# One propagation table with a shared block of fixed rows, and separate 96-wide store tiles in the first dense pass

## The chip, the cores and the metric

The kernel runs on one core of a Trainium2 chip. The metric is the device time of one execution in microseconds; all arithmetic is float32.

## The reference

Four graph layers run one after the other on 50,000 nodes of 96 features with 50,000 edges sorted by destination. Each layer works on `h = relu(layernorm(x))` and adds its result to `x`.

```python
h = relu(layernorm(x));  x = x + attention(h, edges, edge_attr_96)      # L0: 8 heads, sums over edges per destination
h = relu(layernorm(x));  x = x + gated_messages(h, edges, edge_attr_32) # L1: two small networks per edge, update network, layernorm
h = relu(layernorm(x));  x = x + propagate(h, edges)                    # L2: K = 16 rounds
h = relu(layernorm(x));  x = x + gcn(h, edges, edge_weight, W, b)       # L3
# L2, with norm from the in-degrees of both ends and a self loop on each node:
for _ in range(16):
    h = 0.9 * segment_sum(norm * h[row], col) + 0.1 * h_start
```

A node without an incoming edge has only its self loop in L2, so its value never changes over the rounds.

## The kernel before, in words

**Layout.** Every per-node or per-edge list is padded to `ROWS` = 128 x 392 rows: partition p holds 392 consecutive ones, worked on in 49 batches (`NB`) of 8 columns (`J`), that is 1,024 rows or 384 KB a batch. Nodes that have incoming edges are kept a second time in "slots", one per edge position (`SLOTS` = 128 x 400 rows), where the sum of a destination's edges ends up. A table that is gathered from holds first the `ROWS` fixed rows and behind them the `SLOTS` slots. `row_e` holds, for each edge, the row of its source in such a table: below `ROWS` for a node whose value is fixed, `ROWS` + slot for one that changes.

**Stages.** The program is a row of blocks; in each the five queues (SyncE for DMAs, GpSimd for gathers and scatters, TensorE, ScalarE, VectorE) run their own skewed loop (`skewed`: stage function with lag n works on batch t - n in tick t). Semaphores order them; between two blocks all engines meet. SyncE waits for its last stores before it leaves a block. The blocks, with the prefix of their tile names:

- `n`: first layer norm, keys and values (gathers of x).
- `d`, lines 722 to 952, called here the first dense pass: L0 projection of edge features, and, for the nodes as if they had no edge, the L1 update, its layer norm, the sum `x2` and the start value `y0` of L2. GpSimd scatters pointers into `kv_t`. One tile `d_yx`, 192 columns a row, holds `y0` in columns 0 to 95 and `x2` in 96 to 191. The SyncE function `store` writes `x2` to `x2n_t` and `y0` to both tables `y_t[0]` and `y_t[1]`.
- `e0`, `e1`: edge passes of L0 and L1. `e1` stores the start values of the slots into `y_t[1]`.
- `r0` with `d3`: round 0 of L2 (gathers from `y_t[1]`, stores slots to `y_t[0]`) beside the dense part for nodes with fixed values, which loads `y0` from the fixed rows of `y_t[0]`.
- `r`: rounds 1 to 14. GpSimd gathers the source rows of a batch (8 `indirect_dma_start` of 128 rows of 384 bytes) from one table, VectorE scans them, TensorE and ScalarE form the new values in `H`, SyncE stores these to the slots of the other table; a round starts gathering when all stores of the one before have landed.
- `l`, `e3`: round 15 with the L3 product, and the last edge pass with the scatter of the output.

In the first dense pass ScalarE does per tick two groups of 8 `ACTIVATE` of 128x96 (`norm`, `norm2`, line 354), two Gelu (line 876), two copies out of PSUM (`turned`, line 869), two roots (line 341), two table loads and the two copies that set up the scatter (862, 863). TensorE does transposes into `d_te` (line 824), which need the ScalarE copy before them, then the products `d_pu` (line 832), which the Gelu waits for.

`ptr_e` (pointers read back in `e0`) and `src_i` (source indices) are whole-list tiles that nothing uses behind `e0`; `seg` is one that nothing uses behind the first dense pass.

Of the kernel before, what the change touches and what calls it, by code (L numbers as in the profile page):

```python
# [5 lines left out]
P = 128  # L6
N = 50000
D = 96
# [27 lines left out]
KW = 2 * D + WP  # L36
TURN = 8 * P
assert NB % 2 == 1 and 0 < TAIL < CH

# [111 lines left out]
def program(nc, x, src, dst, edge_attr_32, edge_attr_96, edge_weight,  # L151
# [20 lines left out]
    x3s_t = dram("x3s_t", SLOTS, D)  # L172
    y_t = [dram(f"y{k}_t", ROWS + SLOTS, D) for k in range(2)]
    c_t = dram("c_t", SLOTS, D)
# [6 lines left out]
    with outer:  # L181
# [86 lines left out]
        zs = sb("zs", [P, D])  # L268
        ptr_e = sb("ptr_e", [P, CH])
        eps = sb("eps", [P, 1])  # L270
# [451 lines left out]
        with ExitStack() as p0:  # L722
# [32 lines left out]
            with nc.Block() as block:  # L755
                @block.sync
                def _(sp):
# [28 lines left out]
                    def store(b, n, h):  # L786
                        after(sp, s_y0, b + 1)
                        sp.sem_inc(s_turn_s)
                        sp.dma_start(rows_of(x2n_t, 0, b), yx[:, h, :, D:2 * D]).then_inc(s_st[h], 16)
                        for t in y_t:  # L790
                            sp.dma_start(rows_of(t, 0, b), yx[:, h, :, 0:D]).then_inc(s_st[h], 16)
                    skewed(sp, (6, store_e), (2, load_x), (-2, load), (7, store), (0, load_h0), (-2, load_turned))
                    clear_stale(sp)
                    for h in range(K):
                        sp.wait_ge(s_se[h], 16 * OF[h])
                        sp.wait_ge(s_st[h], 48 * OF[h])

# [61 lines left out]
                def _(act):  # L859
# [34 lines left out]
                def _(dve):  # L894
# [33 lines left out]
                    def update(b, n, h):  # L928
                        own3.step(b)
                        after(dve, s_ln, b + 1)  # L930
                        own3.do(V.tensor_tensor(ln[:, h], ln[:, h], r_all[:, 0:1, :].to_broadcast([P, J, D]), ALU.mult))
                        own3.do(V.tensor_tensor(ln[:, h], ln[:, h], r_all[:, 1:2, :].to_broadcast([P, J, D]), ALU.add))
                        own3.end()
                        dve.wait_ge(s_x[h], 48 * (n + 1))
                        dve.wait_ge(s_st[h], 48 * n)
                        V.tensor_tensor(yx[:, h, :, D:2 * D], xs[:, h], ln[:, h], ALU.add).then_inc(s_x2, 1)

                    def stats2(b, n, h):
                        after(dve, s_x2, b + 1)
                        after(dve, s_rn2, b - 3)  # L940
                        after(dve, s_mv2, b)
                        ln_stats(dve, own4, b, yx[:, h, :, D:2 * D], st[:, 1], mv2[:, h], s_mv2)

# [352 lines left out]
        with ExitStack() as p3:  # L1296
# [41 lines left out]
            with nc.Block() as block:  # L1338
                @block.sync
                def _(sp):  # L1340
# [25 lines left out]
                    def store(b, n, h):  # L1366
                        after(sp, s_y0, b + 1)
                        after(sp, s_yn, b + 1)
                        sp.sem_inc(s_turn_s)
                        sp.dma_start(slots_of(x2s_t, 0, b), x2[:, h]).then_inc(s_st[h], 16)  # L1370
                        sp.dma_start(slots_of(y_t[1], ROWS, b), y0[:, h]).then_inc(s_st[h], 16)
                    skewed(sp, (7, edges_only(store_sums)), (3, edges_only(load)), (7, load_xb), (6, load_u),
# [168 lines left out]
                def _(dve):  # L1541
# [136 lines left out]
        with ExitStack() as p5:  # L1678
# [32 lines left out]
            with nc.Block() as block:  # L1711
                @block.sync
                def _(sp):
                    def load(b, n, h):
                        after(sp, s_x3, b - 3)
                        sp.sem_inc(s_turn_s)
                        sp.dma_start(xn[:, h], rows_of(x2n_t, 0, b)).then_inc(s_xn[h], 16)
                        sp.dma_start(yn[:, h], rows_of(y_t[0], 0, b)).then_inc(s_xn[h], 16)

                    def load_own(b, n, h):  # L1720
                        after(sp, s_cy, b - 3)
                        sp.sem_inc(s_turn_s)
                        sp.dma_start(yo[:, h], slots_of(y_t[1], ROWS, b)).then_inc(s_yo[h], 16)

# [5 lines left out]
                    def store_y(b, n, h):  # L1730
                        after(sp, s_y, b + 1)
                        sp.sem_inc(s_turn_s)
                        sp.dma_start(slots_of(y_t[0], ROWS, b), ys[:, h]).then_inc(s_st[h], 16)

# [5 lines left out]
                    def store_out(b, n, h):  # L1740
# [6 lines left out]
                                     ).then_inc(s_so[h], 16)  # L1747
                    sp.dma_start(y_t[0][ROWS:ROWS + SLOTS, :].rearrange("(p j) d -> p j d", p=P)[:, CH + 1:CHS, :],
                                 zeros[:, 0:D].unsqueeze(1).to_broadcast([P, J - 1, D])).then_inc(s_zo, 16)
# [3 lines left out]
                    sp.dma_start(first_slots(y_t[0], ROWS), zs[:]).then_inc(s_zo, 16)  # L1753
                    sp.wait_ge(s_zo, 32)
# [9 lines left out]
                def _(pool):  # L1764
                    def step(b, n, h):
                        after(pool, s_ix, b + 1)
                        after(pool, s_ss, b - 3)
                        gathers(y_t[1], lambda j: g_[:, h, j, :], h, s_g[h])
                    skewed(pool, (0, step))
# [38 lines left out]
                def _(act):  # L1808
                    def slots(b, n, h):
                        gather_rows(act, n, h, row_e, b, s_ix, s_g)  # L1810
                        after(act, s_ss, b - 3)
# [92 lines left out]
        with ExitStack() as p6:  # L1904
# [50 lines left out]
            with nc.Block() as block:  # L1955
                @block.sync
                def _(sp):
                    def one(r, odd):
                        to = y_t[1 - odd]

                        def load(b, n, h):
                            if isinstance(r, int) and r == 0:
                                sp.dma_start(cols(H, b), slots_of(y_t[0], ROWS, b)).then_inc(s_h[h], 16)
                            after(sp, s_up, r * NB + b - 3)
# [3 lines left out]
                        def store(b, n, h):  # L1968
                            if is_last(b):
                                after(sp, s_pv, r + 1)  # L1970
                                sp.sem_inc(s_turn_s)
                                sp.dma_start(slots_of(to, ROWS, b)[:, 0:J - 1, :], cols(H, b)[:, 0:J - 1, :]
                                             ).then_inc(s_st, 16)
                                after(sp, s_s, r * NB + b + 1)
                                sp.sem_inc(s_turn_s)
                                sp.dma_start(slots_of(to, ROWS, b)[:, J - 1, :], cols(H, b)[:, J - 1, :]
                                             ).then_inc(s_st, 16)
# [8 lines left out]
                        sp.dma_start(first_slots(to, ROWS), zs[:]).then_inc(s_zo, 16)  # L1986
                    rounds(sp, one)
# [5 lines left out]
                def _(pool):  # L1993
                    def one(r, odd):
# [5 lines left out]
                        def step(b, n, h):  # L2000
                            after(pool, s_ix, 2 * (r * NB + b) + 2)
                            after(pool, s_ss, r * NB + b + 1 - GB)
                            if not is_last(b):
                                gathers(y_t[odd], lambda j: g_[:, h % GB, j, :], h, s_g[h])
                                return
                            G.sem_inc(s_turn_p)
                            for j in range(J):
                                done = s_g[h] if j < J - 2 else s_end[j - J + 2]
                                G.indirect_dma_start(out=g_[:, h % GB, j, :], out_offset=None, in_=y_t[odd],
                                                     in_offset=bass.IndirectOffsetOnAxis(ap=idx_s[:, h, j:j + 1], axis=0)  # L2010
# [100 lines left out]
        with ExitStack() as p7:  # L2111
# [27 lines left out]
            with nc.Block() as block:  # L2139
                @block.sync  # L2140
                def _(sp):
                    def load(b, n, h):
                        after(sp, s_up, b - 3)
                        sp.dma_start(yo[:, h], slots_of(y_t[0], ROWS, b)).then_inc(s_ld[h], 16)
                        sp.dma_start(cs[:, h], slots_of(c_t, 0, b)).then_inc(s_ld[h], 16)
# [19 lines left out]
                def _(pool):  # L2165
                    def step(b, n, h):
                        after(pool, s_ix, b + 1)
                        after(pool, s_ss, b - 3)
                        gathers(y_t[0], lambda j: g_[:, h, j, :], h, s_g[h])
                    skewed(pool, (0, step))  # L2170
# [40 lines left out]
                def _(act):  # L2211
                    def slots(b, n, h):
                        s_g.wait(act, h, 16 * J * n)
                        A.copy(idx_s[:, h, :], cols(row_e, b)).then_inc(s_ix, 1)
                        after(act, s_ss, b - 3)
# [195 lines left out]
```

## Time and profile before

| | |
|---|---|
| time, median of 3 runs | 11,803.59 us (11,793.79 to 11,810.04) |
| profiled execution, first to last instruction (span) | 11,805.1 us |
| its own time beside the span | the span is the one figure it has; it lies 1.5 us above the median |
| GpSimd busy | 8,514.7 us, 72% of the span |
| TensorE / VectorE / ScalarE busy | 6,807.1 / 6,395.0 / 4,285.7 us |
| DMA moved | 1,804.49 MB, mean 153 GB/s |
| DMA packets | 970,285, of them 412,879 under 512 B |

The profile names engines PE (TensorE), DVE (VectorE), ACT (ScalarE), POOL (GpSimd) and SPq (SyncE's DMA issues). A line number is one of the kernel before. Shares over the whole span mix stages with different limits, so a stage has to be read from its own stretch: the first dense pass lies at about 557 to 1,193 us, rounds 1 to 14 at about 3,160 to 10,185 us.

### The profile page before, as it was taken

Reading aid. Unit: us, or ns where it says so; the run is one execution under the profiler, and the core shown is the slowest. Engines: PE = TensorE matmul, PEld = TensorE weight load, DVE = VectorE, ACT = ScalarE, POOL = GpSimd, SP = SyncE. Lnnn points to the kernel's source line nnn. Section 1 sums busy time; section 2 is a strip of 40 time slices with the busy share of each in tenths; the row PEclk is TensorE's granted clock in tenths of the full one; section 3 lists DMA queues with packets and bytes.
Section 4 is the critical chain, followed back from the end, with each engine's and each line's share of the span. In section 5 each row is a group of like instructions: output and inputs, shape, how many; then the busy total and the mean of one; then the engine's idle time right before and its main releaser. Section 6 shows DMA issues by size and latency. Waiting matters only on the chain. (4 is left out here: it accounts for less than half of the span.)

```text
span 11805.1 us, 140168 instructions
## 1 busy us (share of the span) xinstructions
PE 6807.1 (58%) x20914; PEld 4246.3 (36%) x20914; DVE 6395.0 (54%) x24157; ACT 4285.7 (36%) x14616; POOL 8514.7 (72%) x8690
## 2 busy tenths in 40 slices
PE   4688677966665665655555555655555555672000
PEld 4566566654433332333333323323333333352000
DVE  6577897889744444444444444444444444575443
ACT  5699666978622222222222222222222222373000
POOL 6675765747677777777777777777777777776777
PEclk7666667977777777778777777777777777896555
DMA  7998885668754444444444444444444444573222
GB/s 250 303 252 242 274 275 172 216 217 284 229 157 126 118 113 116 117 113 119 113 115 117 113 119 113 115 117 113 119 113 117 115 113 118 150 233 125 65 67 55
DMA packets 970285, 1804.49 MB, mean 153 GB/s; under 512 B 412879, under 2 KB 423549, under 8 KB 970062
## 3 DMA queue, kind: packets, MB, share of 16 engines
q1 hardware_dynamic: 687725, 1384.14, 34.7%
q0 software_dynamic: 282336, 418.19, 17.0%
q14 instruction: 184, 1.50, 0.0%
q8 instruction: 40, 0.66, 0.0%
HBM read 1070.12 MB, written 738.89 MB: 153 GB/s over the span
## 5 line engine op out<-in xcount | busy, mean ns | idle before, releaser
L365 POOL DMA_INDIRECT r_g<-y_t,idx_s x5768 | 5535.4, 960 | 1947.2 <-issue 1841.0
L1945 DVE SCALAR_TENSOR_TENSOR F<-r_g,scan_s,F 128x96 f32<-128x96 f32 x5488 | 1769.1, 322 | 3974.2 <-DMA r_g<-y_t,idx_s 3147.3
L2074 ACT ACTIVATE H<-r_pu,kc_e 128x96 f32 (+1 forms) x5474 | 1340.2, 355 | 5536.1 <-PE r_pu L2046 5502.2
L2046 PE MATMUL r_pu<-r_S,ident 128*128 128x384 f32 x2688 | 1734.3, 793 | 2797.4 <-DVE r_S L1947 2797.4
L2046 PEld LDWEIGHTS r_pu<-r_S,ident 128*128 128x128 f32 x2688 | 679.4, 278 | 3546.9 <-DVE r_S L1947 3212.0
L1947 DVE SCALAR_TENSOR_TENSOR r_S<-r_S,scan_s,r_g 128x96 f32<-128x96 f32 x5488 | 1719.0, 313 | 0.5
L2028 PE MATMUL r_pu<-H,ident 128*128 (+2 forms) x2744 | 1530.1, 649 | 91.4 <-DMA r_c<-c_t 85.5
L2029 PE MATMUL r_pu<-r_c,ident 128*128 128x384 f32 (+1 forms) x2744 | 1349.0, 579 | 0.0
L2028 PEld LDWEIGHTS r_pu<-H,ident 128*128 128x128 f32 x2744 | 778.1, 284 | 765.1 <-issue 654.6
L2029 PEld LDWEIGHTS r_pu<-r_c,ident 128*128 128x128 f32 x2744 | 666.8, 243 | 559.9 <-issue 361.4
L2335 PE MATMUL e_pc<-e_S,B 128*128 128x96 f32 x2 | 0.7, 474 | 1042.5 <-DVE e_o L2379 1042.5
L365 POOL DMA_INDIRECT e_kv<-kv_t,idx_s x392 | 422.2, 1077 | 244.2 <-issue 126.0
L806 POOL DMA_INDIRECT kv_t<-seg_s,idx_s x392 | 404.1, 1031 | 189.5 <-issue 114.3
L2324 POOL DMA_INDIRECT out<-e_o,e_out_s x393 | 432.2, 1100 | 119.7 <-issue 119.7
L365 POOL DMA_INDIRECT e_g<-z_t,idx_s x392 | 388.7, 992 | 166.0 <-issue 119.2
L365 POOL DMA_INDIRECT e_x<-h_t,idx_s x392 | 379.4, 968 | 134.5 <-issue 107.5
L365 POOL DMA_INDIRECT l_g<-y_t,idx_s x392 | 378.2, 965 | 130.8 <-issue 117.6
L365 POOL DMA_INDIRECT n_x<-in_x,idx_s x392 | 370.2, 944 | 139.8 <-issue 117.5
L2335 PEld LDWEIGHTS e_pc<-e_S,B 128*128 128x128 f32 x2 | 0.5, 310 | 1042.7 <-DVE e_o L2379 1042.7
L2369 DVE TENSOR_TENSOR e_g<-e_g,scan_s 128x768 f32<-128x768 f32 x49 | 47.9, 977 | 553.8 <-DMA e_g<-z_t,idx_s 553.8
L649 PE MATMUL n_kb<-w_kvq,n_hT 97*128 97x192 f32 x784 | 241.6, 494 | 126.0 <-ACT n_hT L682 67.8
L673 ACT ACTIVATE n_h<-n_x,n_rn 128x96 f32<-128x96 f32 x784 | 286.0, 458 | 0.5 <-DVE n_rn L347 0.5
(329 smaller groups left out, 11912.6 us busy)
## 6 DMA issues: line engine op xcount, KB each, us to landing
r_c<-c_t SPq DMA_DIRECT2D x686, 384.0 KB
y_t<-H SPq DMA_DIRECT2D x672, 384.0 KB
r_g<-y_t,idx_s POOLq DMA_INDIRECT x5880
kv_t<-n_kv SPq DMA_DIRECT2D x49, 776.0 KB, 6.9
y_t<-d_yx SPq DMA_DIRECT2D x98, 384.0 KB
agg_t<-e_S SPq DMA_DIRECT2D x49, 416.0 KB, 4.6
x1s_t<-e_xb SPq DMA_DIRECT2D x50, 384.0 KB, 4.8
h_t<-e_h SPq DMA_DIRECT2D x50, 384.0 KB, 5.2
```

The source lines that it names most:

```text
L365: G.indirect_dma_start(out=to(j), out_offset=None, in_=table, in_offset=bass.IndirectOffsetOnAxis(ap=idx_s[:, h, j:j + 1], axis=0)).then_i ...
L649: last = T.matmul(kb[i][:, j % 2, :], hT[:, h, j // 4, j % 4 * P:(j % 4 + 1) * P], w_kvq[:, 0:2 * D], start=True, stop=True)
L673: last = A.activation(hh[:, h, s, j, :], xs[:, h, s, j, :], ACT.Relu, scale=rn[:, h, 0, c], bias=rn[:, h, 1, c])
L806: G.indirect_dma_start(out=kv_t.rearrange("r (a w) -> (r a) w", w=WP), out_offset=bass.IndirectOffsetOnAxis(ap=idx_s[:, h, j:j + 1], axis= ...
L1945: own.add(V.scalar_tensor_tensor(out=F[:, 0:D], in0=g[:, j, :], scalar=scan_s[:, h, j, 1:2], in1=F[:, 0:D], op0=ALU.mult, op1=ALU.add))
L1947: last = V.scalar_tensor_tensor(out=S[:, h % 2, j, :], in0=before, scalar=scan_s[:, h, j, 0:1], in1=g[:, j, :], op0=ALU.mult, op1=ALU.add)
L2028: T.matmul(to, ident[:], cols(H, b)[:, c, :], start=True, stop=False)
L2029: T.matmul(to, ident[:], cs[:, h, c, :], start=False, stop=False)
L2046: last = T.matmul(pu[h % 2][g][:], ident[:], S[:, h % 2, 4 * g:4 * g + 4, :], start=False, stop=True)
L2074: last = A.activation(v[:, j, :], pu[h % 2][j // 4][:, j % 4, :], ACT.Copy, scale=k[:, j, 0:1])
L2324: G.indirect_dma_start(out=out, out_offset=bass.IndirectOffsetOnAxis(ap=dst_s[:, h, j:j + 1], axis=0), in_=ot[:, h, j, :], in_offset=None, ...
L2369: own.do(V.tensor_tensor(g_[:, h], g_[:, h], scan_s[:, h, :, 2:3].to_broadcast([P, J, D]), ALU.mult))
```

## The change

Three edits that belong together.

1. The two tables become one, `y_t`, of `ROWS + 2 * SLOTS` rows: slot region 1 at row 0, the fixed rows at row `SLOTS`, slot region 0 behind them. The fixed rows are stored once. A gather of an odd round reads rows 0 to `SLOTS + ROWS`, one of an even round the whole table.
2. Since the offsets differ now between odd and even rounds, two lists of rows take the place of `row_e` in L2: `row_y[0] = row_e + SLOTS`, and `row_y[1]`, which is that less `SLOTS + ROWS` where the row is a slot. VectorE makes both at the start of `e1`; they lie in `ptr_e` (now of type int32) and `src_i`.
3. In the first dense pass `d_yx` is replaced by two tiles of 96 columns, `d_y0` and `d_x2`, and three stores a batch become two.

```diff
+Y_STATIC = SLOTS
+Y_SLOTS = [SLOTS + ROWS, 0]
+Y_ROWS = [ROWS + 2 * SLOTS, SLOTS + ROWS]
-    y_t = [dram(f"y{k}_t", ROWS + SLOTS, D) for k in range(2)]
+    y_t = dram("y_t", ROWS + 2 * SLOTS, D)
-        ptr_e = sb("ptr_e", [P, CH])
+        ptr_e = sb("ptr_e", [P, CH], I32)
+        row_y = [ptr_e, src_i]
 # first dense pass
-            yx = sb("d1_yx", [P, K, J, 2 * D], F32, p0)
+            y0 = sb("d1_y0", [P, K, J, D], F32, p0)
+            x2 = sb("d1_x2", [P, K, J, D], F32, p0)
-                        sp.dma_start(rows_of(x2n_t, 0, b), yx[:, h, :, D:2 * D]).then_inc(s_st[h], 16)
-                        for t in y_t:
-                            sp.dma_start(rows_of(t, 0, b), yx[:, h, :, 0:D]).then_inc(s_st[h], 16)
+                        sp.dma_start(rows_of(x2n_t, 0, b), x2[:, h]).then_inc(s_st[h], 16)
+                        sp.dma_start(rows_of(y_t, Y_STATIC, b), y0[:, h]).then_inc(s_st[h], 16)
-                        act.wait_ge(s_st[h], 48 * n)
-                        ln_norm(act, b, yx[:, h, :, D:2 * D], yx[:, h, :, 0:D], rn2[:, h], s_rn2, ACT.Relu
+                        act.wait_ge(s_st[h], 32 * n)
+                        ln_norm(act, b, x2[:, h], y0[:, h], rn2[:, h], s_rn2, ACT.Relu
-                        V.tensor_tensor(yx[:, h, :, D:2 * D], xs[:, h], ln[:, h], ALU.add).then_inc(s_x2, 1)
+                        V.tensor_tensor(x2[:, h], xs[:, h], ln[:, h], ALU.add).then_inc(s_x2, 1)
 # e1, VectorE, behind the memset of S
+                    row_f, at_y = seg[:, :, 0], seg[:, :, 1]
+                    first.do(V.tensor_copy(row_f, row_e[:]))
+                    first.add(V.tensor_scalar(at_y, row_f, float(SLOTS), None, ALU.add))
+                    first.do(V.tensor_scalar(row_f, row_f, float(ROWS), None, ALU.is_lt))
+                    first.add(V.tensor_copy(row_y[0][:], at_y))
+                    first.do(V.tensor_scalar(row_f, row_f, float(SLOTS + ROWS), float(-SLOTS - ROWS), ALU.mult,
+                                             ALU.add))
+                    first.do(V.tensor_tensor(at_y, at_y, row_f, ALU.add))
+                    first.do(V.tensor_copy(row_y[1][:], at_y))
 # rounds of L2 (the same in r0 and l): gathers, their rows, stores
-                                gathers(y_t[odd], lambda j: g_[:, h % GB, j, :], h, s_g[h])
+                                gathers(y_t[0:Y_ROWS[odd], :], lambda j: g_[:, h % GB, j, :], h, s_g[h])
-                            A.copy(idx_s[:, h, :], cols(row_e, b)).then_inc(s_ix, 1)
+                            A.copy(idx_s[:, h, :], cols(row_y[odd], b)).then_inc(s_ix, 1)
-                            sp.dma_start(slots_of(to, ROWS, b), cols(H, b)).then_inc(s_st, 16)
+                            sp.dma_start(slots_of(y_t, to, b), cols(H, b)).then_inc(s_st, 16)
```

All other loads and stores of the tables change in their base row alone.

## Rows read from the trace of the kernel before

**Rows 1.** The page: busy time by engine, then busy tenths in 40 slices.

```profile
PE 6807.1 (58%) x20914; PEld 4246.3 (36%) x20914; DVE 6395.0 (54%) x24157; ACT 4285.7 (36%) x14616; POOL 8514.7 (72%) x8690
...
POOL 6675765747677777777777777777777777776777
...
DMA  7998885668754444444444444444444444573222
```

**Rows 2.** The page: the costliest group, the gathers of L2.

```profile
L365 POOL DMA_INDIRECT r_g<-y_t,idx_s x5768 | 5535.4, 960 | 1947.2 <-issue 1841.0
```

**Rows 3.** Windows: stretch, length, busy us of each engine, granted clock, DMA share, GB/s.

```profile
300.00:500.00 200.00, 130.42 (x481) 114.96 (x480) 122.59 (x757) 144.21 (x401) 150.99 (x161) 0.62 0.94 316
700.00:1000.00 300.00, 255.09 (x1079) 197.48 (x1078) 229.54 (x1055) 273.97 (x636) 213.52 (x208) 0.61 0.91 258
1188.00:1192.00 4.00, 0.00 (x0) 0.00 (x0) 0.00 (x0) 0.00 (x0) 0.00 (x0) 0.50 0.99 261
...
4000.00:6000.00 2000.00, 1176.62 (x2373) 610.41 (x2373) 866.26 (x3139) 420.48 (x1950) 1487.72 (x1561) 0.78 0.42 115
```

**Rows 4.** Waits, 640 to 1,130 us: total us, times, longest.

```profile
PE d_te L824 <- ACT d_eaT L869: 71.9, 40, 4.0
DVE d_rn L346 <- ACT d_rn L341: 64.8, 40, 2.4
...
POOL kv_t L806 <- ACT seg_s L863: 44.7, 24, 2.3
ACT L876 <- PE d_pu L832: 41.9, 40, 1.2
...
DVE d_h L913 <- PE d_po L851: 24.0, 24, 1.1
...
DVE d_yx L936 <- DVE d_ln L932: 3.9, 19, 0.2
```

**Rows 5.** Waits of SyncE's queue in the same stretch.

```profile
SPq L101 <- PE d_te L824: 112.1, 38, 3.8
```

**Rows 6.** Timeline of ScalarE, 900 to 926 us: start, us, instruction, idle before.

```profile
904.93 1.28 ACT L876 ACT_TABLE_LOAD   x1 [1.15 <-PE d_pu L832]
...
917.33 1.28 ACT L876 ACT_TABLE_LOAD   x1 [1.15 <-PE d_pu L832]
```

**Rows 7.** DMA, 700 to 1,000 us (first dense pass).

```profile
DMA packets 99730, 77.29 MB, mean 258 GB/s; under 512 B 84707, under 2 KB 84707, under 8 KB 99730
...
y_t<-d_yx SPq DMA_DIRECT2D x48, 384.0 KB
```

**Rows 8.** DMA, 300 to 500 us (first layer norm).

```profile
DMA packets 22093, 63.11 MB, mean 316 GB/s; under 512 B 4810, under 2 KB 4810, under 8 KB 22093
```

**Rows 9.** Timeline, 1,183 to 1,215 us: end of the first dense pass.

```profile
1183.40 2.97 ACT L354 ACTIVATE d_yx<-d_yx,d_rn 128x96 f32<-128x96 f32 x8 [0.60 <-DVE d_rn L347]
1186.46 0.37 SPq L789 DMA_DIRECT2D x2n_t<-d_yx  x1
1186.87 1.93 SPq L791 DMA_DIRECT2D y_t<-d_yx  x2
1192.91 0.29 ACT L360 COPY idx_s<-src_i 128x8 int32<-128x8 int32 x2 [6.54 <-PEq L755]
...
1193.98 0.99 POOL L365 DMA_INDIRECT e_kv<-kv_t,idx_s  x1 [66.90 <-ACT idx_s L360]
```

**Rows 10.** Timeline of VectorE, 1,835 to 1,892 us: end of `e0`, start of `e1`.

```profile
1844.52 0.57 DVE L1255 TENSOR_TENSOR e_none<-e_none,ptr_e 128x392 f32<-128x392 f32 x1
...
1866.84 0.14 DVE L1548 MEMSET e_S<- 128x96 f32 x1
1888.10 0.56 DVE L1555 SCALAR_TENSOR_TENSOR e_g<-e_gate,e_po 128x384 f32<-128x384 f32 x1 [21.12 <-ACT e_gate L1505]
```

**Rows 11.** Timeline of GpSimd, 4,150 to 4,235 us: the border between two rounds.

```profile
4154.45 0.94 POOL L2009 DMA_INDIRECT r_g<-y_t,idx_s  x1 [0.30 <-issue]
4164.02 0.94 POOL L365 DMA_INDIRECT r_g<-y_t,idx_s  x1 [8.63 <-issue]
4165.27 0.94 POOL L365 DMA_INDIRECT r_g<-y_t,idx_s  x1 [0.30 <-issue]
```

More of the change, by code:

```diff
@@ L795, in _ @@
                         sp.wait_ge(s_se[h], 16 * OF[h])
-                        sp.wait_ge(s_st[h], 48 * OF[h])
+                        sp.wait_ge(s_st[h], 32 * OF[h])
                 @block.gpsimd
@@ L934, in update @@
                         dve.wait_ge(s_x[h], 48 * (n + 1))
-                        dve.wait_ge(s_st[h], 48 * n)
-                        V.tensor_tensor(yx[:, h, :, D:2 * D], xs[:, h], ln[:, h], ALU.add).then_inc(s_x2, 1)
+                        dve.wait_ge(s_st[h], 32 * n)
+                        V.tensor_tensor(x2[:, h], xs[:, h], ln[:, h], ALU.add).then_inc(s_x2, 1)
                     def stats2(b, n, h):
@@ L941, in stats2 @@
                         after(dve, s_mv2, b)
-                        ln_stats(dve, own4, b, yx[:, h, :, D:2 * D], st[:, 1], mv2[:, h], s_mv2)
+                        ln_stats(dve, own4, b, x2[:, h], st[:, 1], mv2[:, h], s_mv2)
                     def scale2(b, n, h):
@@ L1370, in store @@
                         sp.dma_start(slots_of(x2s_t, 0, b), x2[:, h]).then_inc(s_st[h], 16)
-                        sp.dma_start(slots_of(y_t[1], ROWS, b), y0[:, h]).then_inc(s_st[h], 16)
+                        sp.dma_start(slots_of(y_t, Y_SLOTS[1], b), y0[:, h]).then_inc(s_st[h], 16)
                     skewed(sp, (7, edges_only(store_sums)), (3, edges_only(load)), (7, load_xb), (6, load_u),
@@ L1717, in load @@
                         sp.dma_start(xn[:, h], rows_of(x2n_t, 0, b)).then_inc(s_xn[h], 16)
-                        sp.dma_start(yn[:, h], rows_of(y_t[0], 0, b)).then_inc(s_xn[h], 16)
+                        sp.dma_start(yn[:, h], rows_of(y_t, Y_STATIC, b)).then_inc(s_xn[h], 16)
                     def load_own(b, n, h):
@@ L1722, in load_own @@
                         sp.sem_inc(s_turn_s)
-                        sp.dma_start(yo[:, h], slots_of(y_t[1], ROWS, b)).then_inc(s_yo[h], 16)
+                        sp.dma_start(yo[:, h], slots_of(y_t, Y_SLOTS[1], b)).then_inc(s_yo[h], 16)
                     def store_c(b, n, h):
@@ L1732, in store_y @@
                         sp.sem_inc(s_turn_s)
-                        sp.dma_start(slots_of(y_t[0], ROWS, b), ys[:, h]).then_inc(s_st[h], 16)
+                        sp.dma_start(slots_of(y_t, Y_SLOTS[0], b), ys[:, h]).then_inc(s_st[h], 16)
                     def store_z(b, n, h):
@@ L1752, in _ @@
                     sp.wait_ge(s_zv, 1)
-                    sp.dma_start(first_slots(y_t[0], ROWS), zs[:]).then_inc(s_zo, 16)
+                    sp.dma_start(first_slots(y_t, Y_SLOTS[0]), zs[:]).then_inc(s_zo, 16)
                     sp.wait_ge(s_zo, 32)
@@ L1767, in step @@
                         after(pool, s_ss, b - 3)
-                        gathers(y_t[1], lambda j: g_[:, h, j, :], h, s_g[h])
+                        gathers(y_t[0:Y_ROWS[1], :], lambda j: g_[:, h, j, :], h, s_g[h])
                     skewed(pool, (0, step))
@@ L1809, in slots @@
                     def slots(b, n, h):
-                        gather_rows(act, n, h, row_e, b, s_ix, s_g)
+                        gather_rows(act, n, h, row_y[1], b, s_ix, s_g)
                         after(act, s_ss, b - 3)
@@ L1958, in one @@
                     def one(r, odd):
-                        to = y_t[1 - odd]
+                        to = Y_SLOTS[1 - odd]
                         def load(b, n, h):
                             if isinstance(r, int) and r == 0:
-                                sp.dma_start(cols(H, b), slots_of(y_t[0], ROWS, b)).then_inc(s_h[h], 16)
+                                sp.dma_start(cols(H, b), slots_of(y_t, Y_SLOTS[0], b)).then_inc(s_h[h], 16)
                             after(sp, s_up, r * NB + b - 3)
@@ L1971, in store @@
                                 sp.sem_inc(s_turn_s)
-                                sp.dma_start(slots_of(to, ROWS, b)[:, 0:J - 1, :], cols(H, b)[:, 0:J - 1, :]
+                                sp.dma_start(slots_of(y_t, to, b)[:, 0:J - 1, :], cols(H, b)[:, 0:J - 1, :]
                                              ).then_inc(s_st, 16)
@@ L1975, in store @@
                                 sp.sem_inc(s_turn_s)
-                                sp.dma_start(slots_of(to, ROWS, b)[:, J - 1, :], cols(H, b)[:, J - 1, :]
+                                sp.dma_start(slots_of(y_t, to, b)[:, J - 1, :], cols(H, b)[:, J - 1, :]
                                              ).then_inc(s_st, 16)
@@ L1985, in one @@
                         after(sp, s_z, r + 1)
-                        sp.dma_start(first_slots(to, ROWS), zs[:]).then_inc(s_zo, 16)
+                        sp.dma_start(first_slots(y_t, to), zs[:]).then_inc(s_zo, 16)
                     rounds(sp, one)
@@ L2008, in step @@
                                 done = s_g[h] if j < J - 2 else s_end[j - J + 2]
-                                G.indirect_dma_start(out=g_[:, h % GB, j, :], out_offset=None, in_=y_t[odd],
+                                G.indirect_dma_start(out=g_[:, h % GB, j, :], out_offset=None, in_=y_t[0:Y_ROWS[odd], :],
                                                      in_offset=bass.IndirectOffsetOnAxis(ap=idx_s[:, h, j:j + 1], axis=0)
@@ L2143, in load @@
                         after(sp, s_up, b - 3)
-                        sp.dma_start(yo[:, h], slots_of(y_t[0], ROWS, b)).then_inc(s_ld[h], 16)
+                        sp.dma_start(yo[:, h], slots_of(y_t, Y_SLOTS[0], b)).then_inc(s_ld[h], 16)
                         sp.dma_start(cs[:, h], slots_of(c_t, 0, b)).then_inc(s_ld[h], 16)
@@ L2168, in step @@
                         after(pool, s_ss, b - 3)
-                        gathers(y_t[0], lambda j: g_[:, h, j, :], h, s_g[h])
+                        gathers(y_t[0:Y_ROWS[0], :], lambda j: g_[:, h, j, :], h, s_g[h])
                     skewed(pool, (0, step))
@@ L2213, in slots @@
                         s_g.wait(act, h, 16 * J * n)
-                        A.copy(idx_s[:, h, :], cols(row_e, b)).then_inc(s_ix, 1)
+                        A.copy(idx_s[:, h, :], cols(row_y[0], b)).then_inc(s_ix, 1)
                         after(act, s_ss, b - 3)
```

2 lines of the change are left out of this document (1 added, 1 removed).

## The prediction

> **What bounds the kernel now.** I read the page first, for the part of each engine and its course over time. GpSimd is the busiest engine, and its tenths stand at 7 through nearly the whole span, while the DMA share falls from 8 or 9 at the start to 4 in the long middle [rows 1]. The costliest group says why: 5,768 gathers of the L2 rounds, 0.96 us each, and before them an idle time put down almost wholly to issue [rows 2]. The timeline shows the same as a beat: inside a round one gather starts every 1.25 us, and 8.63 us lie between the last of a round and the first of the next [rows 11]. Rounds 1 to 14 are thus paced by GpSimd's issue of gathers plus one border each; the DMA engines are at 0.42 there [rows 3].
>
> The change touches data movement in one other place, the first dense pass, so I read that stretch by itself. In its steady part the DMA share is 0.91 at 258 GB/s, the highest share but one in my windows, and ScalarE is busy 273.97 of 300 us [rows 3]. Both look like a limit. The waits decide between them. Over 490 us no engine waits for a transfer. TensorE waits for ScalarE's copy out of PSUM (40 times), ScalarE then for TensorE's products (40 times, 41.9 us, 1.05 us each), VectorE for either of these or itself, and GpSimd's scatter for ScalarE [rows 4]. SyncE itself idles on TensorE 112.1 us [rows 5]. One tick is 12.40 us, the distance of two table loads of the same kind, and both have the same 1.15 us before them [rows 6]. A wait on transfers would vary; this one repeats to the hundredth. The stage is a closed loop of ScalarE (about 11.25 us of work a tick) and TensorE (1.15 us that ScalarE can't cover), and the DMA engines run full beside it without being waited for.
>
> **The change, part by part.**
>
> *Stores of the first dense pass, steady part.* Three stores a batch become two, and their pieces grow from 384 bytes to 3,072, since 8 rows of 96 columns now lie end to end on both sides. That pieces are small today is seen in the stretch: 84,707 of 99,730 packets are under 512 bytes, where the first layer norm, which stores from 96-wide tiles, has 4,810 of 22,093 [rows 7, 8]. Price of one 384 KB store (393,216 bytes): in the stretch where only these stores run, 261 GB/s at share 0.99, so 264 GB/s of full engines and 1.49 us; in whole pieces by the first layer norm, 316 at 0.94, so 336 GB/s and 1.17 us [rows 3]. DMA work a tick is 0.91 x 12.40 = 11.3 us; less 3 x 1.49, plus 2 x 1.17, it becomes 9.2 us, a share of 0.74. On the path this is worth 0: the work that hides it is ScalarE's and TensorE's loop. If that cover were gone (that is, if the wait of ScalarE hung on transfers after all), it would be worth the 1.05 us a tick, 51 us over 49 ticks, and no more, because ScalarE's own work would then set the tick. I take 0 and keep 51 as the far bound of a rival. A loss has no source: same number of instructions on ScalarE, TensorE and VectorE, same shapes, one wait on 32 instead of 48 of stores four batches old.
>
> The Trainium skill, page "DMA: Bandwidth & Descriptors", section "Specifications", asks for pieces of at least 512 B for line rate, so by it today's stores are slow ones. The rows agree in direction and put the price at 1.49 against 1.17 us a store. Taken as a verdict on this stage the rule would promise the 51 us above; by the waits it promises nothing.
>
> *SyncE.* 49 issues fewer (and shorter ones). It waits on TensorE anyway [rows 5]: 0.
>
> *End of the first dense pass.* Here the stores are on the path. ScalarE's last group ends at 1,186.37; the three last stores are issued at 1,186.46 and 1,186.87; nothing computes until ScalarE opens the next block at 1,192.91 [rows 9], and in between the DMA engines are at 0.99 [rows 3]. Of these 6.45 us, 3 x 1.49 = 4.5 us are transfer, 2.0 us issue, landing and the meeting of the engines. After: 2 x 1.17 + 2.0 = 4.3 us. Gain 2.1 us, and the next stage's first gather, at 1,193.98 [rows 9], moves up by as much. Bounds: nothing (if landing and not transfer sets the end) and 4.5 us (if transfer vanished). I take 2.1 us since the share of 0.99 says that transfer fills the gap. Should the pieces not merge, it is 1 x 1.49 = 1.5 us.
>
> *Making the row lists.* Seven VectorE instructions on 128x392. The nearest rows are those at the end of `e0`, at most 0.57 us [rows 10]; seven of them are 4.0 us, with gaps 4.3. They start when the memset of S ends, at 1,866.98, and end by 1,871.3; VectorE's next work comes at 1,888.10 and waits for ScalarE [rows 10]. Cover left: 16.8 us, so 0; with no cover it would be a loss of 4.3. The lists are first read in the block after `e1`.
>
> *Rounds, round 0, last round.* The same number of gathers of 128 rows of 384 bytes, the same copies into `idx_s`, the same stores; only base rows and index values differ. In a round the pace is the 1.25 us of issue [rows 11], which is no matter of the place in memory as long as a gather isn't refused or split: 0. The `d3` part loads `y0` from another base: 0.
>
> **Sum.** 0 - 2.1 + 0 + 0 = -2.1 us against the span of 11,805.1, so 11,803.0; taken off the median instead, 11,801.5. The span lies 1.5 us above the median, inside the 16 us over which the three runs spread, so nothing outside the span can be told apart. I predict 11,801.5 us. 0.2% of the time is 23.6 us, about what a measurement here can tell from no change.
>
> **Rivals.**
>
> 1. *The first dense pass is DMA-bound after all* (faster). For it: share 0.91 and a fifth of that work taken away. Against: not one wait on a transfer in 490 us, and the same 1.15 us in two ticks [rows 4, 6]. The page's rule above points this way. Time: 51 us and the 2.1 of the end, 11,750. Chance 0.08.
>
> 2. *The single table disturbs the borders of the rounds* (slower). Stores of a round now go to the same buffer that it gathers from; if reads and writes there got into each other's way, a gather would land later. Inside a round that is hidden, at a border it isn't: 8.63 us lie there, landing of the last gather and of the last store among them [rows 11]. There are 15 borders (behind rounds 0 to 14). It decides the sign from 23.6 / 15 = 1.6 us a border; if each grew by half, 4.3 us, it would be 65 us: 11,866. Against: the DMA engines are at 0.42 in the rounds [rows 3], and both tables lay in the same memory before. Chance 0.04.
>
> 3. *The pieces don't merge*, so the stores stay small. Then only the third store is saved: 1.5 us instead of 2.1, 11,802. Against: the packets of the first layer norm [rows 8]. Chance 0.04, and it falls within 0.2%.
>
> Left for the forecast: 0.84.
>
> **Range and chances.** Bounds of the known terms: 11,799 (4.5 us gained) to 11,808 (nothing gained, lists uncovered). A median of few runs may lie off by the spread shown, 8 us to either side and as much again for another chip: 11,783 to 11,820. This leaves out rivals 1 and 2, together 0.12. Faster by over 0.2%: rival 1 and a little for what I don't see, 0.09. Slower: rival 2 and a little, 0.05. Within 0.2%: 0.86.
>
> **What the profile of the changed kernel would show.** Packets under 512 B fall by about 150,000 (3 x 49 stores of 1,024 pieces) to some 262,000. The DMA share in the steady part of the first dense pass falls from 0.91 to about 0.74, and the distance of two ticks stays 12.40 us with a wait of 1.15 us for `d_pu`. If the tick shortens to about 11.3 us, rival 1 holds. The gap between the last ScalarE group of that pass and the next block shrinks from 6.5 to about 4.4 us. Seven VectorE instructions stand at 1,865 to 1,870 us, and the first message product comes as late after the block's start as before. Gathers in a round stay 1.25 us apart with 8.6 us at a border; borders of 10 us or more would be rival 2. The forecast is wrong if a change in timing alters TensorE's granted clock (0.61 in that pass, [rows 3]), on which the 1.15 us rest.

## The result

The changed kernel takes 11,840.25 us (median of 6 runs, 11,837.46 to 11,842.39) against 11,801.86 us of the kernel before on the same chip (6 runs, 11,793.79 to 11,811.98). The ratio is 1.0034, with a 95% interval of 1.0024 to 1.0043: slower by 38 us, outside the 0.2% within which I had put it, and outside my range. The forecast was wrong.

The profiled execution of the changed kernel has a span of 11,838.4 us, 33.3 us more than before. Its page, in the parts that answer to [rows 1, 2] (then DMA packets, and the queue that carries instructions):

```profile
PE 6789.6 (57%) x20914; PEld 4254.8 (36%) x20914; DVE 6399.7 (54%) x24164; ACT 4290.8 (36%) x14616; POOL 8515.3 (72%) x8690
...
DMA packets 831552, 1785.50 MB, mean 151 GB/s; under 512 B 261567, under 2 KB 272237, under 8 KB 831294
...
q14 instruction: 219, 1.79, 0.1%
...
L369 POOL DMA_INDIRECT r_g<-y_t,idx_s x5768 | 5535.9, 960 | 1948.0 <-issue 1842.9
```

VectorE has the seven instructions more, the gathers of L2 cost what they did (5,535.9 against 5,535.4 us, idle 1,948.0 against 1,947.2). The loss can't be seen in any of these rows, save that the last queue but one had `q14 instruction: 184` packets before and has 219 now.

To find the place, I take the first gather of each stage as the stage's start. These are the groups of GpSimd's gathers by tile (count, shortest, median and longest ns, first and last start), after:

```profile
L369 POOL DMA_INDIRECT e_kv<-kv_t,idx_s x392: 940/946/1767, 1188.6 to 1788.5; - x196
L369 POOL DMA_INDIRECT e_x<-h_t,idx_s x392: 940/944/1688, 1859.1 to 2520.9; - x196
L369 POOL DMA_INDIRECT r_g<-y_t,idx_s x5768: 938/944/1746, 2626.8 to 10202.4; - x199
L369 POOL DMA_INDIRECT l_g<-y_t,idx_s x392: 938/944/1715, 10224.8 to 10720.6; - x196
```

and two of them before:

```profile
L365 POOL DMA_INDIRECT e_x<-h_t,idx_s x392: 938/944/1730, 1861.3 to 2489.9; - x196
L365 POOL DMA_INDIRECT r_g<-y_t,idx_s x5768: 938/944/1739, 2596.0 to 10170.2; - x199
```

`e1` lasts from the first `e_x` to the first `r_g`: 734.7 us before, 767.7 after, so 33.0 us more. By the same reading of all stages: start of the first dense pass -1.9, that pass -3.5, `e0` +3.2, `e1` +33.0, round 0 and all rounds together +1.2 (on 7,597), `l` +0.9, `e3` +0.4. The sum is the 33.3 us. The whole loss is in `e1`, a stage of which the change touches two things: seven VectorE instructions ahead of its loop, and the base row to which it stores the start values of the slots.

Inside `e1` the waits of VectorE (1,950 to 2,500 us: total us, times, longest) have a row that the kernel before doesn't have:

```profile
DVE e_g L1568 <- issue: 34.1, 7, 5.6
```

and VectorE's timeline shows where it stands, once in 57 us (the next such line is at 2,208.46):

```profile
2146.24 0.55 DVE L1607 TENSOR_TENSOR e_h<-e_h,e_pv 128x384 f32<-128x384 f32 x1
2151.64 1.02 DVE L1568 SCALAR_TENSOR_TENSOR e_g<-e_gate,e_po 128x384 f32<-128x384 f32 x2 [4.85 <-issue]
...
2208.46 1.02 DVE L1568 SCALAR_TENSOR_TENSOR e_g<-e_gate,e_po 128x384 f32<-128x384 f32 x2 [4.95 <-issue]
```

In the kernel before the same pair has no gap between them (2,141.12 and 2,141.69, the first 0.56 us long):

```profile
2141.12 0.56 DVE L1594 TENSOR_TENSOR e_h<-e_h,e_pv 128x384 f32<-128x384 f32 x1 [3.01 <-PE e_pv L1456]
2141.69 1.02 DVE L1555 SCALAR_TENSOR_TENSOR e_g<-e_gate,e_po 128x384 f32<-128x384 f32 x2
```

The releaser of the 4.9 us is "issue", so the profile shows no data or engine that they wait for. They stand where VectorE's loop turns back to its first instruction. The loop in `e1` is run 8 times and so turns 7 times, and 7 x 4.9 us is the 34.1 us, near the 33.0 us by which the stage grew. The queue that carries instructions to the engines points to what VectorE waits for. Over 320 us of the steady loop, 2,110 to 2,430 us, before and then after (packets, MB, share):

```profile
q14 instruction: 1, 0.01, 0.0%
```

```profile
q14 instruction: 27, 0.22, 0.3%
```

Before, one packet comes in all that time; after, nearly five a turn are fetched (27 in 5.6 turns of 57 us), each of 0.22 MB / 27 = 8.1 KB. From the first `e_x` to the first `r_g` it is 60 packets against 26, and the 34 more are nearly the 35 more of the page.

### The profile page after: what moved, and what is told of

It reads as the page before. It is cut to its first block and busy times, and to the rows that moved or that the text cites. A ratio compares the mean times of both kernels' runs of the same rounds, so it can differ in the third digit from the quotient of the medians.

```text
span 11838.4 us, 140113 instructions
## 1 busy us (share of the span) xinstructions
PE 6789.6 (57%) x20914; PEld 4254.8 (36%) x20914; DVE 6399.7 (54%) x24164; ACT 4290.8 (36%) x14616; POOL 8515.3 (72%) x8690
## 2 busy tenths in 40 slices
DMA packets 831552, 1785.50 MB, mean 151 GB/s; under 512 B 261567, under 2 KB 272237, under 8 KB 831294
## 5 line engine op out<-in xcount | busy, mean ns | idle before, releaser
L369 POOL DMA_INDIRECT r_g<-y_t,idx_s x5768 | 5535.9, 960 | 1948.0 <-issue 1842.9
```

The lines of the kernel that those rows point to most:

```text
L369: G.indirect_dma_start(out=to(j), out_offset=None, in_=table, in_offset=bass.IndirectOffsetOnAxis(ap=idx_s[:, h, j:j + 1], axis=0)).then_i ...
```

## The experiments

The theory was that the seven instructions do their harm by where they push the loop behind them. The rivals were that they do it by what they compute, and that the single table or the store tiles do it. All kernels below do the whole work of the reference; `F` is a tile that `e1` doesn't use. "Position" is the number that the loop's first instruction has in VectorE's listing: 2,146 in the kernel before and 2,154 in the changed one; the loop itself is 277 long there. This listing leaves out the instructions that only wait on a semaphore or set one. The compiled kernels have 50 of them inside the loop, so the loop takes 327 places in VectorE's stream, and it begins 7 places further in the changed kernel than before, not 8. The table at the end of this section gives both counts.

**First set: added instructions alone, and the row lists elsewhere.** `b_pad8` is the kernel before with 8 one-column memsets ahead of the loop and nothing else, `b_pad32` with 32, `a_pad32` the changed kernel with 32:

```diff
                     first.do(V.memset(S[:, K - 1, J - 1, :], 0.0))
+                    for i in range(8):
+                        first.add(V.memset(F[:, i:i + 1], 0.0))
```

`a_late` is the changed kernel with the row lists made behind the loop of `e1`:

```diff
-                    row_f, at_y = seg[:, :, 0], seg[:, :, 1]
-                    first.do(V.tensor_copy(row_f, row_e[:]))
...
                     skewed(dve, (6, gated(1)), (5, gated(0)), (9, scale), (6, total), (10, stats2), (8, add(0)),
                            (11, scale2), (8, stats), (9, update), (7, add(1)), total=NX)
+                    row_f, at_y = seg[:, :, 0], seg[:, :, 1]
+                    first.do(V.tensor_copy(row_f, row_e[:]))
...
                     dve.wait_ge(s_y0, NX)
```

Expected of `b_pad8`:

> The kernel before, with 8 one-column memsets of an unused scratch tile on VectorE at the start of e1, ahead of its loop: the loop begins 8 instructions later in VectorE's code, as in the changed kernel (2,154 instead of 2,146), and nothing of the row lists, the single table or the store tiles is there. Theory A (where the loop lies in the code makes VectorE fetch instructions anew in each pass, the trace of the changed kernel has such a stall of about 5 us in each of 7 passes): e1 lengthens by 30 to 35 us and the whole time by as much, ratio to before 1.0025 to 1.0031, instruction packets on queue 14 rise from 184 to about 219. Theory B (the work of the row lists, or the new place of the stores of e1, costs the time): the time stays within 3 us of before, and so do the packets.

Of `b_pad32`:

> The kernel before with 32 such memsets: the loop begins at 2,178. Theory A in the form that a loop of 277 instructions only stalls where it touches one 8 KB block of code (128 instructions of 64 bytes by the fetch size of 8,192 bytes) more: at 32 it has left the bad stretch, so no stall, e1 as before plus at most 3 us, ratio 0.999 to 1.001. Theory A in the form that any added instruction costs: over 30 us slower, like 8. Theory B: as before.

Of `a_pad32`:

> The changed kernel with 32 such memsets behind its row lists: the loop begins at 2,186, all parts of the change and all of its work stay and 2 us of memsets are added. Theory A with blocks: the 33 us of e1 vanish, 11,840 becomes about 11,806 less what the first dense pass gained, so 11,797 to 11,806. Theory B: 11,838 to 11,843, the changed kernel's time or a little more.

Of `a_late`:

> The changed kernel with the seven row-list instructions moved behind VectorE's loop and tail of e1, ahead of its last waits: same instructions, same count, but the loop begins at 2,147. Theory A: 33 us less than the changed kernel, about 11,797 to 11,806 (if the 4 us of the lists lie open at the end of e1, the upper end). Theory B with the row lists' work at the start as cause: also less, but then a_pad32 stays slow; with the stores' place as cause: no change from 11,840.

Measured, against 11,824.09 us of the kernel before (22 runs): `b_pad8` 1.0036 [1.0023, 1.0050] with 218 packets on the page's instruction queue, `b_pad32` 1.0035 [1.0023, 1.0047], `a_pad32` 1.0021 [1.0011, 1.0030], `a_late` 0.9993 [0.9984, 1.0002]. Eight memsets of one column in the kernel before bring the full loss of the change, and its signature. It is somewhat more than theory A expected of them: `e1` takes 773.6 us, 38.9 more than before, where 30 to 35 were expected. The row of VectorE's waits in `b_pad8`, `b_pad32` and `a_pad32`, 1,950 to 2,500 us:

```profile
DVE e_g L1557 <- issue: 33.0, 7, 5.0
```

```profile
DVE e_g L1557 <- issue: 29.4, 7, 4.3
```

```profile
DVE e_g L1570 <- issue: 26.8, 7, 4.2
```

`a_late` has no such row, and one packet in the window from 2,110 to 2,430 us. Its `e1` takes 729.1 us. So the position of the loop, and not the work of the row lists, makes the stall. `b_pad32` and `a_pad32` were misses in one point: I had thought that only some 20 places in 128 were bad ones, and that 32 instructions would leave them. They don't, though the stall is shorter. The 20 follow from the listing's count, 277 - 1 - 2 x 128: from so many starting places a loop of 277 touches four pieces of 128 and not three. With the 327 places of the compiled loop the same working gives 70 bad places in 128, enough for both kernels. No run was made to test this count.

**Second set: how far the bad stretch reaches.** `b_same` is the kernel before as it is, the others have 4, 64 and 128 memsets at the same place:

```diff
+                    for i in range(128):
+                        first.add(V.memset(F[:, i % 64:i % 64 + 1], 0.0))
+                        if i % 64 == 63:
+                            first.settle()
```

> The kernel before, unchanged, for a trace from the same chip as the three beside it. VectorE's loop of e1 begins at instruction 2,146. e1 about 735 us, 27 instruction packets in it, no stall at the loop's turn.

> 4 memsets on VectorE at the start of e1: the loop begins at 2,150, between 2,147 (no stall) and 2,154 (stall). No theory says on which side the border lies; it narrows it. e1 about 735 us with 27 packets, or about 770 us with 61, nothing in between.

> 64 memsets, the loop begins at 2,210. Theory A1 (it counts how the loop lies to the 8 KB pieces, 128 instructions, in which code is fetched): either way, but if it stalls, the stall at the turn is shorter than the 29.4 us at 2,178 and 26.8 us at 2,186. Theory A2 (it counts how much code lies ahead, or that the code became longer): stall of about 5 us a pass, e1 at 770 us or more.

> 128 memsets, the loop begins at 2,274, just one piece of 128 instructions further than in the kernel before. Theory A1: as before, no stall, 27 or 28 packets, e1 about 735 us (the 8 us of memsets are covered). Theory A2: stall, 61 packets or more, e1 at 770 us.

The chip of this set ran every kernel in about 14,100 us, the one before too (14,089.86), so from it I read only the stall and the packets, which need no comparison of times (`b_same` 14,110.78, `b_pad4` 14,113.49, `b_pad64` 14,114.98, `b_pad128` 14,121.90, one run each). VectorE's waits, 2,380 to 3,000 us, of `b_pad4`, then `b_pad64`:

```profile
DVE e_g L1559 <- issue: 23.3, 6, 4.3
```

```profile
DVE e_g L1559 <- issue: 15.9, 6, 3.0
...
DVE e_S L1573 <- issue: 6.9, 6, 1.2
```

In `b_pad64` part of the stop has moved to an instruction further in, `e_S`; in `b_same` and `b_pad128` neither waits for issue in this window. An "issue" wait alone is no sign of fetching, though. `e_x`, which stands behind semaphores for a load and for stores, waits for issue in this set in `b_same` too, with only 2 packets over 400 us:

```profile
DVE e_x L1620 <- issue: 14.2, 7, 4.8
```

Only the waits at the loop's turn come and go with the packets. The instruction queue from 2,500 to 2,900 us has 26 packets in `b_pad4` and `b_pad64` and 2 in `b_same`; in `b_pad128`:

```profile
q14 instruction: 3, 0.02, 0.0%
```

With 128 more instructions the loop is as good again as with none, while 4 to 64 are bad.

**Third set: a good position for the changed kernel, and each other part by itself.** `a_pad120` is the changed kernel with 120 memsets in the same place, which puts its loop at 2,274 = 2,146 + 128, with the row lists still ahead of it:

```diff
+                    for i in range(120):
+                        first.add(V.memset(F[:, i % 64:i % 64 + 1], 0.0))
+                        if i % 64 == 63:
+                            first.settle()
                     row_f, at_y = seg[:, :, 0], seg[:, :, 1]
```

`a_late2` is `a_late` once more. `b_split` is the kernel before with the two store tiles alone, and three stores:

```diff
-            yx = sb("d1_yx", [P, K, J, 2 * D], F32, p0)
+            y0 = sb("d1_y0", [P, K, J, D], F32, p0)
+            x2 = sb("d1_x2", [P, K, J, D], F32, p0)
-                        sp.dma_start(rows_of(x2n_t, 0, b), yx[:, h, :, D:2 * D]).then_inc(s_st[h], 16)
+                        sp.dma_start(rows_of(x2n_t, 0, b), x2[:, h]).then_inc(s_st[h], 16)
                         for t in y_t:
-                            sp.dma_start(rows_of(t, 0, b), yx[:, h, :, 0:D]).then_inc(s_st[h], 16)
+                            sp.dma_start(rows_of(t, 0, b), y0[:, h]).then_inc(s_st[h], 16)
```

`a_wide` is `a_late` with the one tile of 192 columns, so single table and two stores, but small pieces:

```diff
-                        sp.dma_start(rows_of(x2n_t, 0, b), x2[:, h]).then_inc(s_st[h], 16)
-                        sp.dma_start(rows_of(y_t, Y_STATIC, b), y0[:, h]).then_inc(s_st[h], 16)
+                        sp.dma_start(rows_of(x2n_t, 0, b), yx[:, h, :, D:2 * D]).then_inc(s_st[h], 16)
+                        sp.dma_start(rows_of(y_t, Y_STATIC, b), yx[:, h, :, 0:D]).then_inc(s_st[h], 16)
```

> The changed kernel with 120 memsets behind its row lists, all at the start of e1: VectorE's loop begins at 2,274, 128 behind its place in the kernel before. Theory A1 (the place of the loop modulo 128 instructions decides): no stall, 27 or 28 instruction packets in e1, e1 33 us shorter than in the changed kernel, time 0.9990 to 1.0005 of before although there are more instructions than in the changed kernel at 1.0034. Theory A2 (code behind a longer stretch stalls) and theory B (work of the lists at the start, stores of e1 at a new place): as slow as the changed kernel or slower, 1.0025 to 1.0040.

> The same kernel as a_late, for more pairs with before: is the change without the stall faster than the kernel before? Theory A1 with the 3.5 us gained in the first dense pass: ratio about 0.9995, 6 us at most; faster by under 0.1%.

> The kernel before with the two 96-wide tiles of the first dense pass and still three stores to three tables: the third edit without the other two. The forecast's reading: tick unchanged at about 12.4 us, only the end of the pass shorter, by 3 x (1.49 - 1.17) = 1.0 us of transfer; with what the changed kernel showed (end 2.7 us shorter for one store less and larger pieces) 1 to 2 us. Rival 1 of the forecast (transfers pace the pass): 20 us or more. Its pass 630.3 us becomes 628.5 to 629.5, or under 610.

> The kernel of a_late with the 192-wide tile of before in the first dense pass, so two stores in 384-byte pieces: first and second edit without the third. The pass gains 1.5 us at its end (one store of 1.49 us less), 628.5 to 629.5 us; e1 as in a_late, near 730 us with 27 packets; time within 5 us of before. If the single table cost anything in the rounds, it would show here as in a_late: 1 us or more at each border.

Measured, against 11,811.77 us of the kernel before (33 runs): `a_pad120` 11,805.30, 0.9997 [0.9988, 1.0006]; `a_late2` 11,806.91, 0.9995 [0.9986, 1.0004]; `b_split` 11,808.16, 0.9998 [0.9989, 1.0007]; `a_wide` 11,808.06, 0.9999 [0.9990, 1.0009]. The gathers of `a_pad120` by tile show `e1` at 2,585.2 - 1,855.8 = 729.4 us, though more instructions lie ahead of its loop than in any of the bad versions (single executions without a stall lie from 724.9 us, `b_split`, to 736.6, `a_late2`):

```profile
L369 POOL DMA_INDIRECT e_x<-h_t,idx_s x392: 940/944/1697, 1855.8 to 2479.2; - x196
...
L369 POOL DMA_INDIRECT r_g<-y_t,idx_s x5768: 938/944/1692, 2585.2 to 10161.6; - x199
```

In none of these four does VectorE wait for issue at the loop's turn; each has one packet in the window from 2,110 to 2,430 us. All kernels by the position of their loop:

| kernel | position | places further, compiled | wait at the turn, us / turns | packets in the window | `e1`, us |
|---|---|---|---|---|---|
| before | 2,146 | 0 | none | 1 | 734.7 |
| `b_split` | 2,146 | 0 | none | 1 | 724.9 |
| `a_late` | 2,147 | 0 | none | 1 | 729.1 |
| `a_late2` | 2,147 | 0 | none | 1 | 736.6 |
| `a_wide` | 2,147 | 0 | none | 1 | 731.1 |
| `b_pad4` | 2,150 | 3 | 23.3 / 6 | 26 * | * |
| after | 2,154 | 7 | 34.1 / 7 | 27 | 767.7 |
| `b_pad8` | 2,154 | 7 | 33.0 / 7 | 26 | 773.6 |
| `b_pad32` | 2,178 | 31 | 29.4 / 7 | 26 | 764.2 |
| `a_pad32` | 2,186 | 39 | 26.8 / 7 | 30 | 750.5 |
| `b_pad64` | 2,210 | 64 | 15.9 / 6 | 26 * | * |
| `a_pad120` | 2,274 | 127 | none | 1 | 729.4 |
| `b_pad128` | 2,274 | 128 | none | 3 * | * |

(* second set: the window is 400 us long, the waits are those of 6 of the 7 turns, and times aren't compared.)

## Why the prediction was wrong

**The step that failed is "Making the row lists ... Cover left: 16.8 us, so 0".** The term was put at 0, and `e1`, where it lies, grew by 33.0 us. As a reckoning of work it held. The timeline of VectorE after, to be laid beside [rows 10]:

```profile
1864.84 0.38 DVE L1554 CAST seg<-row_e 128x392 f32<-128x392 int32 x1
...
1867.26 0.36 DVE L1561 CAST src_i<-seg 128x392 int32<-128x392 f32 x1
1887.08 0.55 DVE L1568 SCALAR_TENSOR_TENSOR e_g<-e_gate,e_po 128x384 f32<-128x384 f32 x1 [19.46 <-ACT e_gate L1509]
```

The lists take 2.8 us (I had 4.3) and VectorE then waits 19.5 us for ScalarE, as forecast. What I left out is that an instruction also takes up room in the stream. I priced the seven by their running time and asked what covers it; I didn't ask what stands behind them. Behind them is a loop, and moving it by 8 places of the listing (7 of the compiled stream) made VectorE stand 4.9 us at each of its 7 turns. `b_pad8` shows that this alone suffices (1.0036 without any of the change), `a_late` and `a_pad120` that without it the rest of the change costs nothing that the intervals show. A good place comes back about 128 instructions on, in `a_pad120` and `b_pad128`. None of my three rivals was this: of the 0.05 that I gave to a time slower by over 0.2%, 0.04 stood for disturbed borders of the rounds.

The Trainium skill speaks of this on page "Runtime: NRT & Kernel Launch", section "Instruction fetch mechanics": a taken branch whose target isn't in the two blocks of instructions held makes the engine fetch it before it goes on. The trace agrees in kind, 4.9 us of issue wait at the branch's target with packets on the instruction queue, though none of its rows names the fetch as the cause. It doesn't agree in size: the page has blocks of 16 KiB or 256 instructions, and here packets hold 8.1 KB and the loop is good again at 127 and 128 places further. The prediction doesn't use this rule, the only one here that spoke against the change.

**Could the profile of before have warned me?** Its page has the queue of instruction packets (184 of them), but no time hangs on it there; only a window within a loop tells a loop that fetches from one that doesn't.

**End of the first dense pass: right, somewhat small.** The timeline after, beside [rows 9]:

```profile
1180.70 2.97 ACT L358 ACTIVATE d_y<-d_x,d_rn 128x96 f32<-128x96 f32 x8 [0.60 <-DVE d_rn L351]
1183.76 0.33 SPq L794 DMA_DIRECT2D x2n_t<-d_x  x1
1184.14 0.42 SPq L795 DMA_DIRECT2D y_t<-d_y  x1
1187.55 0.30 ACT L364 COPY idx_s<-src_i 128x8 int32<-128x8 int32 x2 [3.88 <-PEq L760]
```

ScalarE's idle time there falls from 6.54 us to 3.88. That is 2.7 us, where I had 2.1. The two parts by themselves: one store less takes off 1.4 us (`a_wide`, 5.16 us idle; I had 1.5), larger pieces with three stores 1.7 us (`b_split`, 4.86 us idle; I had 1.0), so it is the gain from larger pieces that I had too small. The whole pass went from 630.3 to 626.8 us. In single executions of the other kernels it takes 630.1 and 630.5 us without the new stores (`b_pad32`, `b_pad8`), and 626.4 to 627.8 us with them (`a_pad32`, `a_late2`, `a_late`, `a_pad120`).

**Stores in the steady part: right.** Windows, 700 to 1,000 us (columns as in [rows 3]), of after, `b_split` and `a_wide`:

```profile
700.00:1000.00 300.00, 255.01 (x1068) 195.43 (x1068) 230.25 (x1055) 273.39 (x637) 215.06 (x209) 0.61 0.73 223
```

```profile
700.00:1000.00 300.00, 255.93 (x1061) 197.72 (x1062) 228.71 (x1049) 273.62 (x635) 213.79 (x208) 0.60 0.82 256
```

```profile
700.00:1000.00 300.00, 255.10 (x1074) 196.46 (x1074) 229.58 (x1055) 274.04 (x636) 215.04 (x209) 0.61 0.82 225
```

The DMA share is 0.73 (forecast 0.74). With 3 x 1.17 us in place of 3 x 1.49 a tick, `b_split` should have (11.3 - 1.0) / 12.40 = 0.83 and has 0.82. With one store of 1.49 us less, `a_wide` should have 0.79 and has 0.82: the store taken away was worth (0.91 - 0.82) x 12.40 = 1.1 us of DMA work a tick. So my 1.49 us, read where nothing but these stores runs, was too high for the steady part, and that the whole came out at 0.73 is in part luck. `b_split` moves almost the bytes of before (256 against 258 GB/s) in a tenth less of the engines' time. Packets under 512 bytes are 261,567, forecast some 262,000: the pieces merged, and rival 3 is out. ScalarE's busy time is the same in all of them, and its wait for `d_pu` after is what it was in [rows 4]:

```profile
ACT L880 <- PE d_pu L836: 41.6, 40, 1.2
```

A fifth of the stage's DMA work went away and the tick stayed. Rival 1, 51 us faster, is refuted: the pass is 3.5 us shorter in all, 1.4 us in `b_split` and 1.9 us in `a_wide`, and 2.7 of the 3.5 lie at its end.

**The single table: right.** A border between two rounds after, beside [rows 11]:

```profile
4187.78 0.94 POOL L2022 DMA_INDIRECT r_g<-y_t,idx_s  x1 [0.30 <-issue]
4198.05 0.94 POOL L369 DMA_INDIRECT r_g<-y_t,idx_s  x1 [9.33 <-issue]
```

This one is 0.70 us longer, but rival 2 needed 1.6 us at each of 15 borders to show, and the rounds together grew by 1.2 us on 7,597. Rounds differ by more than that between single executions, whatever the tables: with two tables 7,596.8 us before and 7,615.1 in `b_split`, with one 7,598.1 in `a_pad120` and 7,618.6 in `a_late2`. Rival 2 had the right sign by luck: its mechanism isn't in the trace.

**Two slips in the prediction's own figures.** The DMA share of 0.91 is the third of the four in [rows 3], not the highest but one. The range by its own terms, 11,808 and 16 us more, would end at 11,824 and not at 11,820. Neither changes the forecast or reaches the 11,840.25 us measured.

**What the change is worth without the stall.** The forecast was -2.1 us. `a_late`, `a_late2` and `a_pad120` stand at 0.9993, 0.9995 and 0.9997, their medians 4.9 to 6.5 us below the kernel before, and each interval holds 1. So "within 0.2%" was right for the change as it was meant, and a gain of a few us isn't shown. `a_late` is the version to keep: against the changed kernel as given it saves about 0.4% (1.0034 against 0.9993 and 0.9995, each by its comparison with the kernel before).

**Left open.** What sets the border between good and bad, which in the compiled stream lies between 0 and 3 places further than in the kernel before, and where between 64 and 127 places the bad stretch ends. One reading fits all positions in the table: if 128 instructions go into a packet, a loop of 327 touches four such pieces from 70 of the 128 places and three from the others, and only the fourth piece makes it fetch anew. Where the pieces begin isn't on record, so this is argued and not shown. Why nearly five packets are fetched a turn, when by that count the loop lies in three or four. Why the wait shrinks the further the loop moves into the bad stretch (34.1 to 26.8 us over 7 turns). The queue's rows don't name an engine, so that its packets are VectorE's is inferred from who waits. Blocks of another size, or a loop written out in full, weren't tried.

## What to carry to other kernels

An instruction has two prices, its time and its place: before adding even a few cheap ones ahead of a loop, ask where they push it, and put them behind the loop if nothing there needs them. When a stage that the change hardly touches gets longer by the same few us at each turn of a loop, look at the wait put down to issue in front of the loop's first instruction, and at the instruction queue's packets in a window of the steady loop. To tell position from work, add as many dummy instructions to the kernel before.

## What the runs showed of the hardware that I had not expected

- A loop of 327 VectorE instructions (277 without those for semaphores), run 8 times, either fetches nothing while it turns (1 packet in 320 us) or fetches some five packets of 8.1 KB a turn, with a stop of 3.8 to 4.9 us each time (26.8 to 34.1 us over 7 turns; 15.9 us over 6 at the furthest bad position tried, and 6.9 us at a second place). Four one-column memsets ahead of it, three places in the compiled stream, are enough to go from the one to the other, and 128 memsets are good again.
- As far as single executions tell, such a stop reaches the stage's time almost whole. `e1` less its stops is 723.7 to 740.6 us in the four stalled kernels of the table, and `e1` is 724.9 to 736.6 us in the six without a stop. With a spread of 12 us between kernels, the closeness of 34.1 us of stop and 33.0 us of longer stage is in part chance.
- Pieces of 384 bytes in place of 3,072 cost a tenth of the DMA engines' time in this pass (share 0.91 against 0.82 for the same stores), and on the path 1.4 us of 630 in the one execution traced.
